# Fourteen of 812 gathers per layer moved from GpSimd to SyncE, one DMA per row, in a five-layer graph network

## The reference

```python
# first network, 2 layers, width D = 160 (128 features + 32 of a time embedding)
ecat = concat([h[src], h[dst]], axis=-1)
em = relu(layernorm(ecat @ wm.T + bm)) * w[:, None]          # one message per edge
messages = segment_sum(em, dst) / (cnt + 1e-08)
h_new = relu(layernorm(concat([h, messages]) @ wu.T + bu))
h = tw * h_new + (1 - tw) * h
# second network (GATv2), 3 layers, 4 heads of 32
xj = gl[src]                                                 # gl = x @ Wl + bl
e = leaky_relu(xj + gr[dst] + edge_attr @ We, 0.2)
alpha = softmax of einsum(e, att) over the edges of one destination
out = segment_sum(xj * alpha, dst) + bias; batch norm; leaky_relu
```

## Time and profile before

| | us |
|---|---|
| median of 3 runs | 6847.19 |
| lowest and highest | 6838.13, 6868.62 |
| the profiled execution: its own time | 6835.19 |
| its span in the trace | 6833.4 |
| TensorE busy (matmul) | 5228.6 (77%) |
| GpSimd busy | 4656.5 (68%) |
| VectorE busy | 4419.9 (65%) |
| ScalarE busy | 2485.9 (36%) |
| granted TensorE clock, mean | 0.908 |

### The profile page before, as it was taken

One profiled execution on the slowest core, in us unless ns is written; L12 is line 12 of the kernel. 1 busy time (PEld: TensorE's weight loads), 2 busy tenths in 40 slices (PEclk: granted clock), 3 DMA queues, 4 the chain that ended last, 5 costly groups with the idle time before them and its releaser, 6 DMA issues.

```text
span 6833.4 us, 117887 instructions
## 1 busy us (share of the span) xinstructions
PE 5228.6 (77%) x33433; PEld 4525.5 (66%) x33433; DVE 4419.9 (65%) x15206; ACT 2485.9 (36%) x9471; POOL 4656.5 (68%) x4868
## 2 busy tenths in 40 slices
PE   8988851888888788788667777767777776777776
PEld 7555541777777677777556666656666665666675
DVE  5434330777676788877757777765766774777776
ACT  2554420777776587777501111110111111111112
POOL 1777776777776477777357777737777764777772
PEclk9999985999999899999879999978999997989887
DMA  2111111544444355544134444434444443444442
GB/s 65 41 39 39 42 24 57 131 126 126 126 126 112 94 151 151 147 142 142 52 108 136 140 135 132 138 79 129 136 140 133 131 121 93 136 135 135 132 132 68
DMA packets 496381, 755.03 MB, mean 110 GB/s; under 512 B 226141, under 2 KB 358593, under 8 KB 494709
## 3 DMA queue, kind: packets, MB, share of 16 engines
q1 hardware_dynamic: 314500, 425.53, 19.9%
q0 software_dynamic: 180928, 315.57, 19.4%
q10 hardware_dynamic: 320, 6.40, 0.4%
HBM read 647.92 MB, written 98.34 MB: 109 GB/s over the span
## 4 chain that ended last, share of the span: by engine, by line
POOL 20%; PE 15%; DVE 13%; issue 11%; DMA 4%; DVEq 2%; ACT 1%; POOLq 0%; ACTq 0%
POOL AR L577 13%; POOL AR L569 7%; PE PS L1342 5%; DVE AR L1938 4%; PE PS L1358 4%; PE PS L1355 3%; DMA AR<-gtab_d,AR 3%; DVE AR L2007 2%; DVE AR L2018 1%; DVEq L505 1%; DMA AR<-ptab_d,AR 1%; PE PS L1256 1%; PE PS L1232 1%; PE PS L1253 1%; DVE AR L2028 1%
## 5 line engine op out<-in xcount | busy, mean ns | idle before, releaser
L577 POOL DMA_INDIRECT AR<-gtab_d,AR x2436 | 2310.8, 949 | 848.2 <-issue 702.1
L569 POOL DMA_INDIRECT AR<-ptab_d,AR x1624 | 1546.7, 952 | 529.1 <-issue 476.7
L1358 PE MATMUL PS<-AR,ident 128*128 128x140 f32 x4872 | 1115.5, 313 | 246.2 <-DMA AR<-gtab_d,AR 243.0
L1342 PE MATMUL PS<-AR 128*112 128x132 f32 x4872 | 895.5, 318 | 395.8 <-DVE AR L1938 368.7
L1355 PE MATMUL PS<-AR 128*128 x4872 | 1093.5, 309 | 68.1 <-issue 67.9
L1342 PEld LDWEIGHTS PS<-AR 128*112 128x112 f32 x4872 | 704.3, 200 | 542.2 <-DVE AR L1938 259.0
L1358 PEld LDWEIGHTS PS<-AR,ident 128*128 128x128 f32 x4872 | 846.8, 212 | 311.2 <-DMA AR<-gtab_d,AR 309.5
L551 POOL DMA_INDIRECT rec_d<-AR x782 | 771.3, 986 | 371.0 <-issue 235.3
L1023 ACT ACTIVATE AR<-AR 128x448 f32<-128x448 bf16 x609 | 335.3, 570 | 1776.2 <-PE PS L1342 1598.5
L2018 DVE SCALAR_TENSOR_TENSOR AR<-PS,AR 128x280 f32<-128x280 f32 x1218 | 536.9, 445 | 674.9 <-PE PS L1358 672.6
L1256 PE MATMUL PS<-AR,ident 128*128 128x160 f32 x3248 | 790.3, 325 | 223.1 <-DMA AR<-ptab_d,AR 218.3
(11 more groups left out here) (347 smaller groups left out, 7417.4 us busy)
## 6 DMA issues: line engine op xcount, KB each, us to landing
AR<-ste_d SPq DMA_DIRECT2D x404, 512.0 KB
AR<-nbb_d SPq DMA_DIRECT2D x303, 224.0 KB
ste_d<-AR SPq DMA_DIRECT2D x101, 512.0 KB
AR<-gtab_d,AR POOLq DMA_INDIRECT x2436
AR<-ptab_d,AR POOLq DMA_INDIRECT x1624
nbb_d<-AR SPq DMA_DIRECT2D x101, 224.0 KB, 2.4
AR<-key_d SPq DMA_DIRECT2D x94, 224.0 KB
AR<-rec_d SPq DMA_DIRECT2D x812, 8.0 KB
```

The lines of the kernel that those rows point to most:

```text
L569: e.indirect_dma_start(out=XJ1[:, t % 32, :], out_offset=None, in_=tabs_d[0][:, :], in_offset=off).then_inc(done_, 16)
L577: e.indirect_dma_start(out=xj2(t)[:, t % 4, :], out_offset=None, in_=tabs_d[1][:, :], in_offset=off).then_inc(done_, 16)
L1342: x = e.matmul(PS[6 + v_ % 2][0:B, (t % 2) * 132:(t % 2 + 1) * 132], SQ4[:, i % 4, t % 4, :], PX[:, i % 5, t % 4, :, :].rearrange("p h c - ...
L1358: x = e.matmul(o, ident[:, :], xj2(t)[:, t % 4, :], start=False, stop=True, skip_group_check=True)
```

## The change

In each layer the tiles of `SOURCES` (56, 110, 164, ... 758: 14 tiles, one in 54) are left out of GpSimd's loop; in layer 0 only every second of them from the third on (six tiles). SyncE fetches them, one DMA for each of their 128 rows, with the row of the table taken from a register. So it issues 1792 DMAs of one row in each of layers 1 to 4 and 768 in layer 0, and a register load for every 16 of them. `rows_by_step` spreads them over SyncE's steps: in layers 0 and 1 evenly between one row-fetched tile and the next, up to five steps ahead of the tile's own step; in layers 2 to 4 the 128 rows of a tile go over ten steps, from 12 to 2 steps ahead of its own. In layers 0 and 1 the rows land in two slots of their own (`XD`), in the others in the tile's place in `xj2`. The indices must lie in one partition for the register loads, so early in layer 0 SyncE writes the 14 columns of `SRC` to `sidx_d` (1792 single elements) and reads them back as rows. To free semaphores, the nine that counted loads in the sort are used again for the rows.

```diff
@@ -66,6 +66,24 @@
 PART = 132
+SOURCES = list(range(56, 766, 54))
+ROWED = [SOURCES[2::2]] + [SOURCES] * 4
+NTH = [{t: sum(len(r) for r in ROWED[:l]) + n for n, t in enumerate(ROWED[l])} for l in range(5)]
+def rows_by_step():
+    steps = [[[] for _ in range(NQ)] for _ in range(5)]
+    for l in range(5):
+        gap = (ROWED[l][1] - ROWED[l][0]) / 4
+        for t in ROWED[l]:
+            for p in range(128):
+                first, last = (t / 4 - 5 - gap, t / 4 - 5) if l < 2 else (t // 4 - 12, t // 4 - 2)
+                steps[l][max(int(first + (last - first) * p / 128), 0)].append((t, p))
+    return steps
+ROWS_AT = rows_by_step()
 PARTS = [(q, q * PART, min((q + 1) * PART, C)) for q in (4, 5, 0, 1, 2, 3)]
@@ -126,6 +144,7 @@
         key_d = nc.dram_tensor("key_d", (2, C, 128), BF16).ap()
+        sidx_d = nc.dram_tensor("sidx_d", (len(SOURCES), 128), I32).ap()
         tabs_d = [nc.dram_tensor("ptab_d", (NP, D), F32).ap(), nc.dram_tensor("gtab_d", (NP, GW), F32).ap()]
@@ -208,6 +227,8 @@
         KTC = carve(128)
+        XD = carve(2 * D).rearrange("p (g f) -> p g f", f=D)
+        free0 = cur[0]
         cur[0] = u0
@@ -223,7 +244,8 @@
-        assert cur[0] <= AREA - 4 * T - TK - NB, cur[0]
+        free0 = max(cur[0], free0)
+        assert free0 + 128 <= AREA - 4 * T - TK - NB, free0
         cur[0] = AREA - 4 * T - TK - NB
@@ -233,6 +255,14 @@
         CR = carve(NB, B)
+        def source_row(n):
+            if n < 12:
+                p, c = 64 + 32 * (n // 6), AREA - T - NB + n % 6 * 128
+            else:
+                p, c = 32 * (n - 12), free0
+            return p, c
@@ -348,7 +378,6 @@
         s_pool = sem("s_pool")
-        s_ld = [sem(f"s_ld{i}") for i in range(3)]
         s_sc = [sem(f"s_sc{i}") for i in range(8)]
@@ -358,8 +387,8 @@
         s_ste = [sem(f"s_ste{i}") for i in range(4)]
-        s_r2 = [sem(f"s_r2{i}") for i in range(4)]
         s_o = sem("s_o")
+        s_xi = sem("s_xi")
         s_vown, s_sown, s_pown = sem("s_vown"), sem("s_sown"), sem("s_pown")
@@ -369,8 +398,9 @@
             sem(n) for n in ("s_tr", "s_tev", "s_ot", "s_gm", "s_rk", "s_cv", "s_cb", "s_hb", "s_hs", "s_xp", "s_xr", "s_row", "s_koh", "s_hp"))
-        s_key = [sem(f"s_key{i}") for i in range(2)]
-        s_bc = [sem(f"s_bc{i}") for i in range(2)]
+        s_loads = [sem(f"s_loads{i}") for i in range(9)]
+        s_ld, s_key, s_bc, s_r2 = s_loads[0:3], s_loads[3:5], s_loads[5:7], s_loads[7:9]
+        SORTED = [48, 96, 96, 128, 96, 32 * len(LOADS[0::2]), 32 * len(LOADS[1::2]), 32, 32]
         s_e, s_att, s_lin, s_aff = (sem(n) for n in ("s_e", "s_att", "s_lin", "s_aff"))
@@ -439,9 +469,20 @@
+        taken = [0] * 32
+        GATHERED = {}
+        for layer_ in range(5):
+            for t_ in range(T):
+                if t_ not in NTH[layer_]:
+                    taken[t_ % 32] += 16
+                    GATHERED[layer_, t_] = taken[t_ % 32]
         def gath_sem(layer, t):
-            g = layer * T + t
-            return s_g[g % 32], 16 * (g // 32 + 1)
+            if t in NTH[layer]:
+                n = NTH[layer][t]
+                return s_loads[n % 9], SORTED[n % 9] + 2048 * (n // 9 + 1)
+            return s_g[t % 32], GATHERED[layer, t]
@@ -498,6 +539,39 @@
             return cache["v"][t % 16]
+        def source_of(cache, n, p):
+            if cache.get("g") != (n, p // 16):
+                r0, c0 = source_row(n)
+                _, vs = nc.values_load_multi_w_load_instructions(
+                    AR[r0:r0 + 1, c0 + p // 16 * 16:c0 + p // 16 * 16 + 16].bitcast(I32), engines=[mybir.EngineType.SP], min_val=0, max_val=NP - 1,
+                    skip_runtime_bounds_check_because="an edge's source, so 0 to N - 1")
+                cache["g"], cache["v"] = (n, p // 16), vs
+            return cache["v"][p % 16]
+        def rows_of_step(e, w, layer, i, cache):
+            if i >= NQ or not ROWS_AT[layer][i]:
+                return
+            w.wait_ge(s_tab, 64 * (layer + 1) if layer < 2 else 128 + 80 * (layer - 1))
+            for t, p in ROWS_AT[layer][i]:
+                n = NTH[layer][t]
+                if p == 0 and layer < 2 and n >= 2:
+                    l2 = layer if n - 2 in NTH[layer].values() else layer - 1
+                    w.wait_ge(s_sum, pair_at(l2, next(t2 for t2, n2 in NTH[l2].items() if n2 == n - 2) // 2))
+                if p == 0 and layer >= 2 and t >= 4 * NXJ:
+                    w.wait_ge(s_px, quad_at(layer - 2, t // 4 - NXJ))
+                if p == 0:
+                    k = SOURCES.index(t)
+                    w.wait_ge(s_xi, 16 + 16 * 4)
+                    cache["k"] = k
+                x = source_of(cache, cache["k"], p)
+                if layer < 2:
+                    o, d = XD[p:p + 1, n % 2, :], tabs_d[0]
+                else:
+                    o, d = xj2(t)[p:p + 1, t % 4, :], tabs_d[1]
+                e.dma_start(o, d[bass.ds(x, 1), :]).then_inc(s_loads[n % 9], 16)
@@ -561,6 +635,8 @@
                 for t in range(T):
+                    if t in NTH[layer]:
+                        continue
                     off = bass.IndirectOffsetOnAxis(ap=SRC[:, t:t + 1], axis=0)
@@ -661,10 +737,10 @@
                         e.dma_start(R2T[:, 2 * i:2 * i + 2, :, :].rearrange("p j l w -> p j (l w)"),
-                                    rect[256 * i:256 * i + 256, :].rearrange("(j x) f -> x j f", j=2)).then_inc(s_r2[i], 16)
-                    e.dma_start(R2T[0:C - 768, 6, :, :].rearrange("p l w -> p (l w)"), rect[768:C, :]).then_inc(s_r2[3], 16)
+                                    rect[256 * i:256 * i + 256, :].rearrange("(j x) f -> x j f", j=2)).then_inc(s_r2[i // 2], 16)
+                    e.dma_start(R2T[0:C - 768, 6, :, :].rearrange("p l w -> p (l w)"), rect[768:C, :]).then_inc(s_r2[1], 16)
                     w.wait_ge(s_pe, PM["exp"])
-                    own = {}
+                    own, taken_ = {}, {}
                     for i in range(NQ + 8):
@@ -672,6 +748,18 @@
                                 e.dma_start(SQB[:, i % 6, kk, B:128], rec_d[bass.ds(x * 128, 128), 3:19]).then_inc(s_rg[i % 6], 16)
+                        if i == 2:
+                            w.wait_ge(s_dve, DV["src"])
+                            e.dma_start(sidx_d.rearrange("t l -> l t"),
+                                        SRC[:, SOURCES[0]:SOURCES[-1] + 1:SOURCES[1] - SOURCES[0]],
+                                        allow_slow_non_contiguous=True).then_inc(s_xi, 16)
+                        if i == 5:
+                            w.wait_ge(s_xi, 16)
+                            for n0, n1 in ((0, 6), (6, 12), (12, 13), (13, 14)):
+                                p0, c0 = source_row(n0)
+                                e.dma_start(AR[p0:p0 + 1, c0:c0 + (n1 - n0) * 128].bitcast(I32),
+                                            sidx_d[n0:n1, :].rearrange("t l -> (t l)").unsqueeze(0)).then_inc(s_xi, 16)
+                        rows_of_step(e, w, 0, i, taken_)
                         if i == 16:
@@ -689,6 +777,8 @@
                             read_ste(e, w, 1, g8)
+                            rows_of_step(e, w, 1, 2 * g8, taken_)
+                            rows_of_step(e, w, 1, 2 * g8 + 1, taken_)
                         if g8 == 8:
@@ -754,6 +844,7 @@
                     o8 = g8 - 7
+                    rows_of_step(e, w, l + 2, 2 * g8, taken_)
                     if o8 >= 0:
@@ -762,6 +853,7 @@
                             nl_sem(l, 2 * o8)[0], 16)
+                    rows_of_step(e, w, l + 2, 2 * g8 + 1, taken_)
             for g in range(7):
@@ -1196,7 +1288,7 @@
                         x1, lo, hi = min(128, C - 128 * j), 128 * j, min(128 * j + 156, T)
-                        w.wait_ge(s_r2[j // 2], 16)
+                        w.wait_ge(s_r2[j // 4], 32)
                         for f in range(3):
@@ -1253,7 +1345,8 @@
                                 w.wait_ge(*gath_sem(l, t))
-                                x = e.matmul(o, ident[:, :], XJ1[:, t % 32, :], start=False, stop=True, skip_group_check=True)
+                                x = e.matmul(o, ident[:, :], XD[:, NTH[l][t] % 2, :] if t in NTH[l] else XJ1[:, t % 32, :],
+                                             start=False, stop=True, skip_group_check=True)
                             b = OWN[l].get(j)
...
                                 f0, f1 = (0, 128) if u % 2 == 0 else (128, D)
```

## The result

The changed kernel takes 7475.5 us at the median (7462.3 to 7480.8, 4 runs), the kernel before, with one more run, 6845.9: ratio 1.0909, 95% interval 1.0887 to 1.093. Forecast were 7430 us, slower, and a range from 6880 to 7810.

A forecast was written before the change was run, and what follows sets the result against it. GpSimd's gathers were taken to bound the kernel, SyncE after the change: 12 (layer 0) + 103 (layer 1) + 468 (layers 2 to 4) = +583 on 6835.19 gives 7418, forecast as a 7430 us median; range 6880 to 7810.

The forecast's parts named there:

- What bounds the kernel: Whole kernel: GpSimd's gathers, one per 1.25 us, set the pace by a small margin; with rows SyncE becomes the bound.
- The cost of a row: SyncE's time per one-row DMA with register work and its share of a load: r = 0.54 us, from 0.48 to 0.59.
- Layer 0: SyncE needs 839 us against 814 over 162 steps, covered by its lead; the index turn leaves +12 us.
- the lead of 25: SyncE runs six steps, 30 us, ahead of TensorE; less about 5 for a read's landing, 25 us of lateness are absorbed.
- The index turn: Early layer 0: writing 1792 four-byte elements takes 6 to 18 us and holds up line 674's DMAs; +12 us.
- Layer 1: SyncE needs 1058 us against 930 over 185 steps; 25 are absorbed, then TensorE waits for STE: +103 us.
- Layers 2 to 4: Rows in ten-step bursts plus a new wait per tile use up SyncE's lead: +156 us a layer, +468 in all.
- My cycle: Layers 2 to 4: 13.5 steps, one row-fetched tile to the next, take 81.4 us instead of 67.5.
- The wait for the weighting: Layers 2 to 4: before a tile's first row SyncE waits for the step 29 before the tile's own; about 7 us.
- Who waits: TensorE or its weight loads wait for STE, VectorE and ScalarE behind them; GpSimd waits hundreds of us a layer.
- That SyncE keeps up: Rival, layers 2 to 4: r under 0.466 us and a free wait make the kernel faster, 6770 to 6810 us; chance 0.10.
- Only the average counts: Rival, layers 2 to 4: the wait is hidden, +116 a layer, 7310 us; inside the forecast case of chance 0.78.

The follow-up runs named there:

- e3: Changed kernel with the same one-row DMAs from fixed table rows, without register operations, moves or register loads; 8581.4 us, 1.0089 of the kernel before.
- e8: Changed kernel with all gathers back on GpSimd, only the turn of the indices left; 8567.3 us, 0.9999 of the kernel before.
- e4: Kernel before, without row DMAs, plus only the waits for the weighting in layers 2 to 4; 8491.9 us, 0.9986 of the kernel before.
- e6: Changed kernel with the rows of layers 2 to 4 issued four steps later; 9843.5 us, 1.1488 of the kernel before.

## Why the prediction was right, step by step

**What bounds the kernel, and that SyncE would be the next bound:** right. The chain after shows it, and e3 takes the register work of the rows away, and with it the loss.

**The cost of a row, r = 0.54:** too high. The DMA took 0.228 instead of 0.28, the register operation 0.037 instead of 0.055; the register load 1.227 instead of 0.973. Sum 0.49, near the lower end of 0.48. With the gaps to its neighbours it is 0.50 to 0.51: in each layer I added up SyncE's instructions in the trace from the first row to the last, each with the gap before it and its wait kept apart, and hold my sums against that.

**Layer 0, forecast +12, measured +50.** From first row to last SyncE took 897 us: 391 for the rows, 453 for line 674 (now 750) with its loads, 33 for writing STE, and 19 of waits. The 162 steps are 808 us at TensorE's pace before (1012.3/203 = 4.99), so 89 are too much, and less the lead of 25 some 64 remain, against 50. The mis-sized term is line 674, 384 in my sum: its DMAs with their register operations took 0.60 us each, not 0.532, and its 40 loads in this stretch 1.7 in the mean, not 0.973. Why such a load takes longer there was not tried. The index turn, +12, was dear: its issue took 0.43 us and e8 bounds the whole. How the delay gets to TensorE my sum had not said; here it is not STE but the edge attributes, a wait that is absent from the same view before:

```profile
PE PS L1308 <- DMA AR<-rec_d: 155.2, 93, 4.2
```

**Layer 1, forecast +103, measured +71.** From first row to last SyncE took 1007 us: 901 for the rows where I had 968, 99 for its other reads and writes where I had 90, and 6 of waits. I held it against GpSimd's 5.03 us a step, while TensorE, which starts 25 us after GpSimd, needed 998.2/203 = 4.92, 910 us for 185 steps instead of 930. So 103 - 67 + 9 + 6 + 20 = +71: the mechanism and the lead of 25 us are as forecast, and the terms were too dear by 32.

**Layers 2 to 4, forecast +156 each, measured +171, +173, +164.** Three sizes were off, against each other. In layer 2 nine cycles with the wait took 82.9 us each in the mean, from 3749.58 to 4495.45:

```profile
3749.58 5.27 SPq L574 DMA_DIRECT2D AR<-gtab_d  x13
...
4495.45 3.50 SPq L574 DMA_DIRECT2D AR<-gtab_d  x8
```

My cycle was 81.4. The 128 rows took 63.9 us, not 69.1. The other work is 13.5 x 0.53 = 7.1, not 5.3: I had left it out of the 3.5 steps without rows. The wait for the weighting, priced at 7 us a cycle, is 118.8/10 = 11.9; why it is longer I did not isolate, but TensorE, which it waits for, runs at the lower clock after its own waits, and I had put the matmuls at nothing. The two cycles ahead of the first wait took 74.5 us each. So the total of +583 was hit within 8%, of +637 between the spans, because a cheaper row and a dearer wait and turn cancelled; the mechanism is what the runs bear out, the sizes were luck in part.

**Who waits:** right for layers 2 to 4. I named TensorE's wait for STE first, and that is where the chain goes; ScalarE's wait for the one-hots is longer (568 us) and stands beside it. Of the signs, these came as written: SyncE's wait before the STE reads 58.8 (forecast under 150), GpSimd's for free slots or line 2100 198, about one wait for the weighting a tile (10 or 11 in a layer). These did not: rows without a load are 0.407 us apart and not 0.48, and a step took 5.27 us in layer 1, where I had written 5.8, and 5.23 in layer 0, where I had written 5.0 to 5.2; 5.8 for layer 1 did not fit my own +103 either, which makes 5.5.

**The rivals.** That SyncE keeps up needed r = 0.466; measured was 0.49, only 5% over it, and yet the loss is 9%: the condition that the wait costs nothing, which stood beside it, failed too. Estimated from the trace, SyncE's work over the steps with rows of layer 2, without the wait, is 1107 - 121 = 986 us against 925 and a lead of 25: 36 of the 171. "Only the average counts" (7310 for r = 0.54) fails with the idle 119 us. The figure in the Trainium skill, "DMA: Bandwidth & Descriptors", of 512 sequencer cycles per DMA for the generations before the one that passage is about (an estimated 0.43 us) is not borne out: 0.228 us. Its advice in "Rules for kernel authors" to coalesce small transfers is: 128 one-row DMAs cost SyncE 128 x 0.49 = 63 us, where GpSimd's single gather of the same rows took 1.25.

## What to carry to other kernels

An engine that waits 90% of its time is not free by that much: add up issue, register work and loads per item and hold the sum against the pace of the path, over the stretch in which the items lie and not over the kernel. What is saved (1.25 us a tile) must be held against what it costs on the other queue (63 us a tile): such a trade can pay only while the other queue is idle for all of it, and here it was a loss as soon as it wasn't, because short and urgent reads stand in the same queue. A wait placed in a queue was free while little stood behind it (e4) and cost nearly its length when the engine had become the bound (e6: 79 us of wait less, 70 us of the layer less). And the longest wait in a list need not be the one that delays: ask whether the chain goes through it.

## What the runs showed of the hardware that I had not expected

- The issue of a DMA of one row with a register address took 0.228 us at the median over 7936 of them, against 0.333 for one of 128 rows on the same queue.
- The same load of 16 registers took SyncE 0.973 us at the median before and 2.011 (51 loads; 1.7 in the mean of the steps with rows) when one-row DMAs were issued between its DMAs; the loads for the rows took 1.227.
- After 9.7 us without work TensorE's granted clock was 0.52 for some 4 us, then 1.00 again; over the span it fell from 0.908 to 0.862 with the waits, and the same matmuls were busy 122 us longer.
- On the chips of the experiments single register operations and issues took up to 1.4 us, with unchanged medians; the change there costs 17% instead of 9%. The row instructions of layer 2 took 1160 us in all, gaps included, instead of 755; that a queue with many short instructions pays for each pause fits this, and what the pauses are is open.
